# Sine and gate products of a two-block kernel: from VectorE to a ScalarE copy and a GpSimd product

## The reference

```python
# block 1: linear attention with rotary position, per head of 16 channels
q, k = elu(q) + 1, elu(k) + 1
k = k * softmax(SCALE * q.mean() @ k) * N
q_rope = q * cos + rotate_every_two(q) * sin      # theta_shift
k_rope = k * cos + rotate_every_two(k) * sin
z = 1 / (q @ k.mean() + 1e-6)
res = (q_rope @ (k_rope.T @ v)) * z               # + depthwise 5x5 conv of v, * o, projected
# block 2: mamba on four groups of 32 channels
h = exp(d_t * A) * h + (d_t * u_t) * B_t          # scan over the 256 pixels, 16 states
y = einsum('nds,ns->nd', h, C_t) + u * Dp
y = y * silu(z)                                   # gate
y = y @ W_out.T                                   # + skip, layer norm, projection
```

## Time and profile before

| | us |
|---|---|
| median of 3 runs | 405.52 |
| lowest and highest of them | 405.22, 407.69 |
| the profiled execution, its own time | 402.74 |
| its span, first to last instruction | 400.9 |
| VectorE busy (336 instructions) | 299.3 |
| TensorE busy | 278.6 |
| ScalarE busy | 212.5 |
| GpSimd busy (120 instructions) | 203.1 |

### The profile page before, as it was taken

One profiled execution on the slowest core, in us unless ns is written; L12 is line 12 of the kernel. 1 busy time (PEld: TensorE's weight loads), 2 busy tenths in 40 slices (PEclk: granted clock), 3 DMA queues, 4 the chain that ended last, 5 costly groups with the idle time before them and its releaser, 6 DMA issues.

```text
span 400.9 us, 5253 instructions
## 1 busy us (share of the span) xinstructions
PE 278.6 (69%) x1756; PEld 121.6 (30%) x1756; DVE 299.3 (75%) x336; ACT 212.5 (53%) x374; POOL 203.1 (51%) x120
## 2 busy tenths in 40 slices
PE   2676864838579588957896789668857676754735
PEld 1433432313134233423442244224422212311212
DVE  1543132247989969996999699969997989999960
ACT  2424358147746855685568546864764637453201
POOL 0021111015655586558564946484659466956650
PEclk9998799575959958995799579967995858665755
DMA  8303322292297438642964296519651665392000
GB/s 264 100 20 83 80 76 81 85 398 105 75 277 223 158 83 273 223 171 66 286 195 198 56 288 190 211 45 284 196 222 35 215 187 207 116 353 108 0 13 13
DMA packets 27938, 62.73 MB, mean 156 GB/s; under 512 B 3088, under 2 KB 15632, under 8 KB 27920
## 3 DMA queue, kind: packets, MB, share of 16 engines
q1 hardware_dynamic: 27632, 61.90, 47.6%
q10 hardware_dynamic: 288, 0.61, 0.4%
HBM read 55.50 MB, written 6.99 MB: 156 GB/s over the span
## 4 chain that ended last, share of the span: by engine, by line
DVE 37%; PE 26%; issue 13%; ACT 9%; DMA 8%; POOL 3%; SPq 1%; DVEq 1%; POOLq 1%; ACTq 0%
DVE hst L921 17%; DVE BIN L914 10%; PE F L431 3%; DVE QK L832 3%; PE DU L456 3%; ACT dec L656 3%; PE F L345 3%; DMA dlt<-delta_scratch 2%; PE F L377 2%; PE Y L471 2%; PE F L390 2%; PE F L329 2%; DMA CCs<-cc 1%; DMA bc_scratch<-bc 1%; PE F L341 1%
## 5 line engine op out<-in xcount | busy, mean ns | idle before, releaser
L740 POOL TENSOR_TENSOR hst<-hst,Cs 128x1024 f32<-128x1024 f32 x64 | 150.8, 2358 | 120.7 <-DVE hst L921 120.7
L921 DVE TENSOR_TENSOR_SCAN hst<-dec,BIN 128x1024 f32<-128x1024 f32 x64 | 146.0, 2281 | 4.5 <-ACT dec L656 2.8
L914 DVE TENSOR_TENSOR BIN<-DU,Bs 128x1024 f32<-128x1024 f32 x64 | 78.6, 1228 | 18.3 <-PE DU L456 8.3
L656 ACT ACTIVATE dec<-dlt,negA 128x1020 f32<-128x1020 f32 x64 | 72.5, 1140 | 27.3 <-DMA dlt<-delta_scratch 14.8
L471 PE MATMUL Y<-hst,CCs 128*32 128x256 f32 x512 | 51.0, 478 | 25.4 <-POOL hst L740 25.4
L377 PE MATMUL F<-V,wpatch 128*32 128x256 f32 x512 | 36.0, 413 | 1.2 <-DVE xl L876 1.2
L471 PEld LDWEIGHTS Y<-hst,CCs 128*32 128x32 f32 x512 | 14.2, 124 | 58.6 <-POOL hst L740 36.4
L431 PE MATMUL F<-xs,W1s 128*64 128x512 f32 x16 | 14.0, 970 | 24.1 <-DVE cor L883 24.1
L456 PE MATMUL DU<-du,CCs 32*128 32x512 f32 x64 | 24.8, 858 | 6.9 <-DVE BIN L914 6.9
L699 POOL TENSOR_TENSOR t<-QK,W0s 128x512 f32<-128x512 f32 x8 | 8.7, 1092 | 28.2 <-DVE QK L832 28.2
L534 ACT ACTIVATE e_qk<-F,W0s 128x256 f32<-128x256 f32 x16 | 7.6, 475 | 23.8 <-PE F L329 23.8
(11 more groups left out here) (136 smaller groups left out, 455.4 us busy)
## 6 DMA issues: line engine op xcount, KB each, us to landing
Bs<-bc_scratch SPq DMA_DIRECT2D x32, 512.0 KB, 5.6
Cs<-bc_scratch SPq DMA_DIRECT2D x32, 512.0 KB, 6.3
dlt<-delta_scratch SPq DMA_DIRECT2D x16, 512.0 KB, 5.4
V<-v_scratch SPq DMA_DIRECT2D x32, 200.0 KB, 4.2
XN<-xn_scratch SPq DMA_DIRECT2D x32, 128.0 KB, 2.7
delta_scratch<-delta SPq DMA_DIRECT2D x16, 128.0 KB, 4.2
v_scratch<-vpad SPq DMA_DIRECT2D x8, 211.5 KB, 2.2
xn_scratch<-XN SPq DMA_DIRECT2D x8, 129.5 KB, 2.1
```

Source lines behind the costliest of these rows:

```text
L656: af(dec[g % 4][:, :, 1:T], dlt[2 * j + g // SG][:, :, 1:T], ACT.Exp, scale=negA[:, g:g + 1]).then_inc(S("decay_ready"), 1)
L740: tt(hst[g % 4][:], hst[g % 4][:], Cs[g % SG][:], ALU.mult).then_inc(S("hc_ready"), 1)
L914: v.tensor_tensor(flat(BIN[:]), flat(DU[:]), Bs[g % SG][:], ALU.mult).then_inc(S("b_ready"), 1)
L921: v.tensor_tensor_scan(hst[g % 4][:], flat(dec[g % 4][:]), flat(BIN[:]), 0.0, ALU.mult, ALU.add).then_inc(S("h_ready"), 1)
```

## The change

Both products that VectorE made out of PSUM now take two steps. ScalarE copies the PSUM bank to SBUF (`F0` to a new tile `rS`, `Y` to a new tile `yS`), and GpSimd makes the product from the copy. The tiles `t2` and `y2` and the numbers are the same. Who may overwrite the banks changes too: TensorE's L350 now waits for `rot_copied` and its L468 for `y_copied`, both set by ScalarE's copies.

```diff
-        t1, t2 = sb("t1", [P, 2, T]), sb("t2", [P, 2, T])
+        t1, t2, rS = (sb(n, [P, 2, T]) for n in ("t1", "t2", "rS"))
...
-                pe.wait_ge(S("t2_ready"), b + 1)
+                pe.wait_ge(S("rot_copied"), b + 1)
...
-                    wait(pe, "y2_ready", b)
+                    wait(pe, "y_copied", b)
...
+                yield 20
+                act.wait_ge(S("rot_done"), b + 1)
+                wait(act, "t2_ready", b)
+                nc.scalar.copy(flat(rS[:]), F0[:]).then_inc(S("rot_copied"), 1)
...
             def back(b, j):
+                yield 4
+                act.wait_ge(S("y_summed"), GROUPS * (b + 1))
+                wait(act, "y2_ready", b)
+                nc.scalar.copy(flat(yS[:]), Y[:]).then_inc(S("y_copied"), 1)
...
                 yield 21
+                pool.wait_ge(S("rot_copied"), b + 1)
+                tt(t2[:], rS[:], wt("sin").unsqueeze(1).broadcast_to([P, 2, T]), ALU.mult).then_inc(S("t2_ready"), 1)
...
-                yield from ()
+                yield 5
+                pool.wait_ge(S("y_copied"), b + 1)
+                wait(pool, "xc2_done", b)
+                tt(flat(y2[:]), flat(yS[:]), flat(zs[j][:]), ALU.mult).then_inc(S("y2_ready"), 1)
...
-                yield 21
-                dve.wait_ge(S("w0_loaded"), 16)
-                dve.wait_ge(S("rot_done"), b + 1)
-                v.tensor_tensor(t2[:], F0[:].rearrange("p (a t) -> p a t", a=2),
-                                wt("sin").unsqueeze(1).broadcast_to([P, 2, T]), ALU.mult).then_inc(S("t2_ready"), 1)
...
-                yield 4
-                dve.wait_ge(S("y_summed"), GROUPS * (b + 1))
-                v.tensor_tensor(flat(y2[:]), Y[:], flat(zs[j][:]), ALU.mult).then_inc(S("y2_ready"), 1)
```

More of the change, by code:

```diff
@@ L102, in block_kernel @@
         hst = [sb(f"hst_{j}", [P, 4 * T]) for j in range(4)]
-        y2 = sb("y2", [P, 2, T])
+        y2, yS = sb("y2", [P, 2, T]), sb("yS", [P, 2, T])
         sq2, lr2, rr2, xl2 = (sb(n, [P, T]) for n in ("sq2", "lr2", "rr2", "xl2"))
```

## The result

The changed kernel takes 421.8 us (median of 4 runs, 421.0 to 427.6); the kernel before, run beside it, 406.6 (4 runs, 405.2 to 408.9). The ratio is 1.036, with a 95% interval of 1.029 to 1.043: slower by 15.2 us. The forecast was 420.0, in a range of 409 to 427.

A forecast was written before the change was run, and what follows sets the result against it. VectorE had the largest share of the chain of waits, 37% of the span (TensorE 26%). The terms, 3.2 + 1.4 + 4.8 + 2.2 + 3.1 - 0.2 = +14.5 us, took the 405.5 median to 420.0, range 409 to 427.

The forecast's parts named there:

- Term 1: Rotation, periods 1 to 4: copy and GpSimd's products delay L363, so KVM comes 0.8 us later each, +3.2 in all.
- would be ready for KVM at 204.4: Rotation, middle period: VectorE, 0.7 us ahead without t2, is ready for KVM at 204.4 and waits until 205.9.
- if VectorE did not wait before KVM: Rotation, periods 0 to 4: an idle wait of about 1.4 us for L363 was expected; its absence would refute the forecast.
- Term 2: Rotation in period 0, TensorE at the lower clock at first: the same delay, some 0.6 us larger, +1.4 (+0.8 to +2.5).
- Term 3: Gate, periods 1 to 4: GpSimd's y2 comes in between L817 and kraw, 1.2 us each, +4.8 (0 to +5.1).
- the rival by which VectorE keeps its turn: Gate, periods 1 to 4: kraw goes before GpSimd's y2, so nothing is lost there; 415.2 us, chance 0.18.
- Term 4: Prologue, where no scan covers anything: delayed rotations cost +2.2 in one front and +3.1 in the next.
- the second front's transposes: Prologue, second rotation: transposes start at 47.2 instead of 44.97 behind the copy and GpSimd's products, +2.2 (+1.8 to +3).
- the third front's rl: Prologue, third rotation: the copy stands behind a table load, so rl starts +1.7 or +3.1 later by TensorE's clock; +3.1 taken.
- Term 5: Periods 5 to 7 and the end: y2 off VectorE gives -1.4, the end costs +1.25; sum -0.2 (-0.9 to +0.6).
- I count it twice, -1.4: Periods 5 to 7: y2's 0.68 us comes back in two of three, as in period 6 cor meets lnu.
- The fourth rival: Rotation, five periods: TensorE's clock falls in the new pauses, up to 3.5 us more each; 437 us, chance 0.08.

The follow-up runs named there:

- the rotation alone: The changed kernel with the gate product back on VectorE, so only the rotation product is moved: 420.1 us, ratio 1.033.
- the gate alone: The kernel before with only the gate product moved to GpSimd through ScalarE's copy of Y: 413.9 us, ratio 1.017.
- copy behind VectorE's product: The kernel before plus a ScalarE copy of F0 that nobody reads, with L350 waiting for it; t2 stays on VectorE: 419.5 us, ratio 1.037.
- copy ahead of rr: Only the rotation product moved against the kernel before, with ScalarE's copy of F0 placed ahead of lr and rr: 406.4 us, ratio 1.002.
- the gate behind kraw: The changed kernel with GpSimd's y2 also waiting until kraw of the same unit is done: 421.3 us, ratio 1.038.

## Why the prediction was right, and where a step of it failed

**The sum.** +14.5 forecast, +15.2 timed, +14.4 from the stages. The mechanism it named first, losses in the rotation and at kraw that outweigh what VectorE is spared, is what the rotation alone (+3.3%) and the gate alone (+1.7%) show. The two don't add up: 5.0% apart, 3.6% together; in periods 1 to 4 they are 3.4 and 4.9 us apart and 6.7 together, where the forecast took 3.2 + 4.8 = 8.0. Period 1 of the changed kernel shows the two losses by themselves, for there TensorE runs as in the kernel before (L345 takes 1.13 us): from unit 2 to unit 5 every BIN starts 1.06 or 1.07 us later than before, by kraw, and the rest of the period adds 0.60, by the rotation; 40.72 + 1.07 + 0.60 = 42.39. That is 1.67 us where the forecast had 2.0.

**Term 1 had the right size and left out one of the two operands that came late.** The step that failed is this: without t2 VectorE "would be ready for KVM at 204.4", and what comes late is L363. I had not looked at what stands right ahead of KVM: xl (L899), which waits for ScalarE's second rr. VectorE and ScalarE of the kernel before:

```profile
203.55 1.23 DVE L914 TENSOR_TENSOR BIN<-DU,Bs 128x1024 f32<-128x1024 f32 x1
204.69 0.47 DVE L899 SCALAR_TENSOR_TENSOR xl<-F,W1s,rr 128x256 f32<-128x256 f32 x1
```

```profile
204.13 0.42 ACT L649 ACTIVATE rr<-lr 128x256 f32<-128x256 f32 x1
```

The table counts from the start of the first rr. "KVM by rr" adds to the start of the second rr its 0.42, the 0.03 after which xl starts wherever it has waited, and xl's 0.40. "KVM by L363" adds to its start its 0.71 and the 0.04 after which KVM starts where KVM itself has waited (period 3 of the changed kernel: L363 ends at 261.70, KVM starts at 261.74).

| | second rr starts | KVM by rr | L363 starts | KVM by L363 | KVM started |
|---|---|---|---|---|---|
| before | 6.46 | 7.31 | 5.64 | 6.39 | 7.42 |
| copy behind VectorE's product | 7.17 | 8.02 | 6.33 | 7.08 | 8.02 |
| changed | 7.17 | 8.02 | 7.20 | 7.95 | 8.02 |
| copy ahead of rr | 5.87 | 6.72 | 5.92 | 6.67 | 6.72 |

Before, VectorE's own queue was last: xl started right behind BIN, and rr had 0.11 us to spare (it ended at 204.55 and could have let xl start at 204.58; xl started at 204.69). So taking t2 off VectorE could win 0.11 us here, not 0.7, as long as rr comes when it does. The copy, put between the two rr, moves the second by 0.71 through L350 and lz, and KVM by 0.60. GpSimd's late product would let KVM start by L363 only 0.07 us sooner than by rr. So the path of the forecast was late as well. It adds nothing in the three periods of the changed kernel in which L345 takes 1.13 us, and 0.37 us in period 3, where L345 takes 2.07 and KVM itself waits 0.28 us for L363. Its sign of being wrong, "if VectorE did not wait before KVM", came true in those three periods; the wait stood before xl.

The copy behind VectorE's product shows that a late rr is enough for the loss. That the late product alone would cost as much follows from the table and was not run. The copy ahead of rr takes both away, since it also lets QKR start 1.3 us sooner than in the changed kernel (0.94 us later against rr than before), so the place of the copy is what decides, for the one path and for the other.

The size owes something to luck. The forecast was 0.8 us a period; where TensorE runs as before it is 0.6, or 2.4 us in four. With the rotation alone L345 took 2.08 us in three of the periods, which lose 1.7, 1.1 and 0.8, and the fourth wins 0.2; the term foresaw none of that, and its 3.2 lies near their sum, 3.4.

**Term 2** (+1.4): +1.5 measured, within its bounds.

**Term 3** (+4.8): the mechanism is right. y2 came in ahead of kraw in each of four places, at 1.07 us each on kraw (1.2 was said); the rival by which VectorE keeps its turn is out. The Trainium skill (page SBUF — State Buffer, section Who interferes with whom) has whole instructions exclude each other by issue order, and by this rule y2 goes first. The trace agrees: kraw takes 1.48 us behind y2, which started 0.25 us ahead of it. That the gate alone comes to +4.9 is luck: in three of its periods the 1.07 is won back ahead of the rotation, and a slower L345 loses 0.9 there, by a step that the term doesn't have. Nor is the term a saving that can be had back: with kraw at 0.41 again the kernel was not faster.

**Term 4** (+5.3): +5.5 over the profiles, 5.4 by the ratio of the run that undoes it, both uncertain by more than 1 us. Piece by piece, from the end of L345: the second front's transposes come 2.1 us later (2.2 said), the third front's rl 2.5 (3.1 said; L350 took 0.81 and L428 1.91 us, where both had been taken at the lower clock, 1.19 and 2.0). The first front costs 0.06.

**Term 5** (-0.2, bounds to +0.6): +0.7. The end costs what was said: L441 starts 3.13 us after L471 instead of 1.90, +1.23. What failed is "I count it twice, -1.4": period 5 is 0.2 shorter and period 6 is 0.2 longer. Undoing the gates there gave nothing measurable either, so the size of this term lies within the scatter from profile to profile (period 6 took 31.2 to 34.0 us with the code of before). Whether it is a loss at all stays open.

**TensorE's clock.** The fourth rival, clock falls in the rotation's pauses, had 0.08, and as a loss of 17 us it didn't come. But the forecast treated the clock as fixed elsewhere, and that it came out so near was luck: the lost gain of the run with the gate behind kraw, and the unequal periods of the rotation alone and of the gate alone, go with shifts of when TensorE runs at 1.2 and when at 2.4 GHz (no run shows what moves them), and in the prologue its matmuls ran at either speed from the same code.

## What to carry to other kernels

Before an instruction is moved, read for the instruction that comes next not only whom it waits for, but what the one ahead of it on the same queue waits for, and how many hundredths of a microsecond each operand has left: here a step with 0.11 us of slack stood one row above the one that I worked through. A copy that feeds another engine is cheap if it stands in a wait that its engine already has (406.4 us) and dear behind the next two instructions of that engine's queue (420.1). And where two engines shut each other out of SBUF, first try to turn one input into a PSUM tile: on another product of this kernel that won 1.8%, while handing two products to the other engine lost 3.6%.

## What the runs showed of the hardware that was not expected

- The exclusion hits the smallest VectorE instructions as well: `nv`, 128x1, took 0.22 us alone and up to 2.29 us beside GpSimd's 128x1024 product.
- Turning one of VectorE's two SBUF tiles into a PSUM tile was enough to end it. The same instruction ran in 0.48 us beside the product that held it 2.55 us before.
- The same program reaches its first BIN at 81.9 or 87.9 us from the same code, while 11 of its 12 loop periods (1 to 4 in three profiles) agree within 0.2 us. A first part of the difference, 2.66 us, comes from matmuls at half speed (L329: 1.10 or 2.05 us) while the granted clock reads 1.00 in both profiles. A single profile of before and one of after would have put the prologue's loss at 8.7 us; over four of each it was 5.5.
- A gain ahead of a stretch of matmuls can change which of them run at 1.2 GHz: 2.3 us won by unit 4 of a period were lost by its end.
